# First two groups of a layer multiplied by x in one VectorE instruction, and two whole chunks in place of four

## The chip, the cores and the metric

The kernel runs on one core of a Trainium2 chip. The metric is the device time of one execution in microseconds, the median of several runs. All five engines of the core share its SBUF; the matrix results lie in PSUM.

## The reference

The input x has 512 samples of 39 fields with 32 components each. Three layers follow one another; each forms all products of the fields with the hidden rows of the layer before, component by component, multiplies them by a weight matrix, adds a bias and takes the positive part. Half of the 200 outputs of layers 0 and 1 is hidden input of the next layer, the other half goes to the result; layer 2 gives all 200. The result is summed over the 32 components.

```
hidden = x
for i in range(3):
    z = einsum('bmd,bnd->bmnd', x, hidden).reshape(B, -1, D)
    cur = relu(einsum('bcd,co->bod', z, Ws[i]) + bs[i][None, :, None])
    hidden, direct = (cur[:, :100], cur[:, 100:]) if i < 2 else (cur, cur)
    finals.append(direct)
y = concatenate(finals, axis=1).sum(-1)
```

All inputs and outputs are 32-bit floats.

## The kernel before

A **unit** is one of the 4 tiles of 128 samples at one of the 32 components: 128 units. For each unit the products of a layer are laid out in **chunks** of 128 rows by 128 samples: 7 chunks in layer 0, 31 chunks in each of layers 1 and 2 (39 fields by 100 hidden rows). The 31 chunks are worked on in four **groups** of 8, 8, 8 and 7 (`GROUP`, `GROUPS`, `group_chunks`).

Each group, and layer 0 as one, is a numbered batch that passes through four steps:

- VectorE multiplies hidden rows by x into one slot of `z` (three slots, `RING`) (`product12`, for layer 0 `product0`), and counts the semaphore `product`.
- ScalarE copies the slot, rounded, into `z_high` (`highs`; four buffers), after `product` has reached the batch.
- VectorE subtracts `z_high` from `z` into `z_low` (`lows`; three buffers). It waits for `high` of this batch, then for `freed`: the multiplication three batches before must have ended.
- TensorE multiplies each chunk twice (`multiply`): `z_high` by the high and low halves of the weights (400 columns, L812), and `z_low` by the high half (200 columns, L813). This makes a nearly full-precision product out of a faster number format.

`WHOLE` chunks at the front of layer 2 don't take this way. They are multiplied in full 32-bit form, once, from `z_whole` and `w_whole` (L805); so group 0 of layer 2 has 4 whole and 4 split chunks, and its `highs` and `lows` run over 4 chunks. `z_whole` lies in front of the three slots of `z`, so that one instruction writes the whole and the split part when the batch has slot 0.

The order on each engine is written out by hand in `period`. A period takes layer 1 of unit n, layer 0 of unit n+2 and layer 2 of unit n-1, nine batches in all. On VectorE, P is a product, L a `lows`, the number is the batch within the period:

```
P0 L(-1) P1 L0 P2 L1 P3 L2 sums2 P4 directs L3 P5 L4 P6 L5 P7 L6 P8 L7 sums
```

Batches 0 to 3 are layer 1, 4 is layer 0, 5 to 8 are layer 2. TensorE takes the batches in their order, two transposes at the period's end. ScalarE takes `highs` 0 to 8 in order; before `highs` 3 it makes the hidden rows of layer 2 (`second_half2`, `hidden(1, ...)`), before `highs` 5 those of layer 1 (`hidden(0, ...)`). `slot_read` makes a product wait until the `lows` three batches before has ended. SyncE loads x, repeated over the partitions, for the next unit: after P5 has ended the chunks of group 0 (`load_xb`: L284 for partitions 0 to 95, L291 for the rest), after P6 those of group 1, and so on; layer 1's product of the next unit waits for them on `xb_in[g]`. There are two buffers of x.

In the last two units layer 0 is absent, so that slots fall otherwise; there, and in the closing part after the loop, group 0 of layer 2 is multiplied in two instructions (L464 and L468).

Of the kernel before, what the change touches and what calls it, by code (L numbers as in the profile page):

```python
# [10 lines left out]
P = 128  # L11
# [41 lines left out]
TAIL_AT = GROUP * (GROUPS - 1)  # L53


WHOLE = 4


RING, HIGH_RING = 3, 4
# [9 lines left out]
def group_chunks(g):  # L69
    return min(GROUP, CHUNKS - GROUP * g)  # L70


def split_from(layer, g):
    return WHOLE if (layer, g) == (2, 0) else 0


def split_chunks(layer, g):
    return group_chunks(g) - split_from(layer, g)


# [21 lines left out]
def cin_kernel(nc, r_x, W0, W1, W2, b0, b1, b2, out):  # L102
# [6 lines left out]
    with ExitStack() as ctx:  # L109
# [81 lines left out]


        def stage(l, g):
            at, n = g % 2 * STAGED, split_chunks(l, g)
            return mixed[:, at:at + n * O].rearrange("p (c o) -> p c o", o=O)

        z_all = z_both
# [27 lines left out]

        def piece(l, g):
            at = GROUP * g + split_from(l, g) - (WHOLE if l == 2 else 0)
            return w_split[l][:, at:at + split_chunks(l, g), :]

        def load_w(queue, l, g, w, bias):  # L230
            k = GROUPS * (l - 1) + g
            skip, n = split_from(l, g), split_chunks(l, g)
            a = GROUP * g + skip
            wt, row = w.tensor, HID * O
            st = stage(l, g)
            if skip:
                queue.dma_start(w_whole[0:MAIN, :, :], bass.AP(wt, 0, [[O, MAIN], [row, skip], [1, O]])).then_inc(w_whole_in, 16)
                queue.dma_start(w_whole[MAIN:P, :, :], bass.AP(wt, CHUNKS * row, [[O, P - MAIN], [row, skip], [1, O]])).then_inc(w_whole_in, 16)
            queue.dma_start(st[0:MAIN, :, :], bass.AP(wt, a * row, [[O, MAIN], [row, n], [1, O]])).then_inc(w_in[k], 16)
            if g < GROUPS - 1:  # L240
                queue.dma_start(st[MAIN:P, :, :],
                                bass.AP(wt, (CHUNKS + skip) * row + 32 * g * O, [[O, P - MAIN], [row, n], [1, O]])).then_inc(w_in[k], 16)
            else:
                queue.wait_ge(stage_ready, l)
                full = F // TAIL_CHUNKS
                at = MAIN + TAIL * full
                for t in range(TAIL):
                    queue.dma_start(st[MAIN + t:at:TAIL, 0:TAIL_CHUNKS, :],
                                    bass.AP(wt, (MAIN + t) * O, [[TAIL_CHUNKS * row, full], [row, TAIL_CHUNKS], [1, O]])).then_inc(w_in[k], 16)
                queue.dma_start(st[at:at + TAIL, 0:F - TAIL_CHUNKS * full, :],  # L250
                                bass.AP(wt, TAIL_CHUNKS * full * row + MAIN * O, [[O, TAIL], [row, F - TAIL_CHUNKS * full], [1, O]]))\
                     .then_inc(w_in[k], 16)
                queue.dma_start(st[ONES_ROW:ONES_ROW + 1, 0, :], bass.AP(bias.tensor, 0, [[O, 1], [1, O]])).then_inc(w_in[k], 16)
# [160 lines left out]
        def _(dve):  # L414
# [25 lines left out]
            def product0(u, number, slot):  # L440
# [3 lines left out]
                dst = z[0:L0_ROWS, slot % RING, 0:L0_CHUNKS * T].rearrange("p (c t) -> p c t", t=T)  # L444
                nc.vector.tensor_tensor(dst, left, x_right[0:L0_ROWS, :, :], ALU.mult).then_inc(product, 1)  # L445

            def product12(layer, u, par, g, number, slot):
                slot_read(number)
                if g == 0:
                    dve.wait_ge(hid_in[layer], u + 1)  # L450
                if layer == 1:
                    dve.wait_ge(xb_in[g], xb_count(u))
                    if isinstance(u, int) and u < 2:
                        dve.wait_ge(repeats_in[u], HALVES * Q)
                n, c0 = group_chunks(g), GROUP * g
                dst = z[:, slot % RING, 0:n * T].rearrange("p (c t) -> p c t", t=T)
                left = hid[layer][:, par, g, :].unsqueeze(1).to_broadcast([P, n, T])
                if split_from(layer, g):

                    if not (isinstance(u, int) and u == 0):  # L460
                        dve.wait_ge(whole_used, u)
                    dst = z_both[:, 0:n * T].rearrange("p (c t) -> p c t", t=T)
                    if slot % RING:
                        nc.vector.tensor_tensor(dst[:, 0:WHOLE, :], left[:, 0:WHOLE, :], xb[par][:, 0:WHOLE, :], ALU.mult)  # L464
                        n, c0 = n - WHOLE, WHOLE
                        dst = z[:, slot % RING, 0:n * T].rearrange("p (c t) -> p c t", t=T)
                        left = left[:, WHOLE:, :]
                nc.vector.tensor_tensor(dst, left, xb[par][:, c0:c0 + n, :], ALU.mult).then_inc(product, 1)  # L468

            def lows(number, slot, rows, n):  # L470
                dve.wait_ge(high, number + 1)
# [96 lines left out]
            def period(r, d, n, base, sl):  # L568

                par = d % 2  # L570
                second, final = (r, d) == (0, 1), (r, d) == (TILES - 1, D - 1)
                a, b = layers_ended(r, d)

                def slot(p):
                    return sl + p

                product12(1, n, par, 0, base, slot(0))
                if not second:
                    lows(base - 1, slot(-1), P, group_chunks(3))
                product12(1, n, par, 1, base + 1, slot(1))  # L580
                lows(base, slot(0), P, group_chunks(0))
                if second:
                    sums(0, 2, ended(0), 2)
                    low_piece(5, 2, 0)
                product12(1, n, par, 2, base + 2, slot(2))
                lows(base + 1, slot(1), P, group_chunks(1))
                product12(1, n, par, 3, base + 3, slot(3))
                if second:
                    low_piece(6, 2, 1)
                    dve.wait_ge(w_low_done, 7)  # L590
                    stage_zeros(2)
                lows(base + 2, slot(2), P, group_chunks(2))
                if not second:
                    sums2(n - 2)
                q = 4
                if a == 0:
                    product0(n + 2, base + 4, slot(4))
                directs(r, d, n)
                if a == 0:
                    lows(base + 3, slot(3), P, group_chunks(3))  # L600
                    q = 5
                if second:
                    low_piece(7, 2, 2)
                product12(2, n - 1, 1 - par, 0, base + q, slot(q))
                if a == 0:
                    lows(base + 4, slot(4), L0_ROWS, L0_CHUNKS)
                else:
                    lows(base + 3, slot(3), P, group_chunks(3))
                product12(2, n - 1, 1 - par, 1, base + q + 1, slot(q + 1))
                lows(base + q, slot(q), P, split_chunks(2, 0))  # L610
                product12(2, n - 1, 1 - par, 2, base + q + 2, slot(q + 2))
                lows(base + q + 1, slot(q + 1), P, group_chunks(1))
                if second:
                    low_piece(8, 2, 3)
                if final:
                    sums(a, b, ended(n), n + 2)
                product12(2, n - 1, 1 - par, 3, base + q + 3, slot(q + 3))
                lows(base + q + 2, slot(q + 2), P, group_chunks(2))
                if not final:
                    sums(a, b, ended(n), n + 2)  # L620
# [11 lines left out]

            at = first(UNITS)
            lows(at - 1, at - 1, P, group_chunks(3))
            product12(2, UNITS - 1, 1, 0, at, at)
            sums2(UNITS - 2)
            for g in range(1, GROUPS):
                product12(2, UNITS - 1, 1, g, at + g, at + g)
                lows(at + g - 1, at + g - 1, P, split_chunks(2, g - 1))
            lows(at + 3, at + 3, P, group_chunks(3))  # L640
            dve.wait_ge(s_in, ended(UNITS - 1))
# [10 lines left out]
        def _(act):  # L652
# [73 lines left out]
            def period(r, d, n, base, sl):  # L726
# [33 lines left out]
                if turn:  # L760
                    for bank in range(X_BANKS):
                        turned_x(r + 1, bank)
                highs(base + q + 1, slot(q + 1), P, group_chunks(1))
                if second:
                    high_piece(2, 3)
                if final:
# [29 lines left out]
        @block.tensor  # L796
        def _(pe):
            def multiply(layer, number, slot, g=0):
                c0, n = (0, L0_CHUNKS) if layer == 0 else (GROUP * g + split_from(layer, g), split_chunks(layer, g))
                rows, chunks = (L0_ROWS, L0_CHUNKS) if layer == 0 else (P, CHUNKS)  # L800
                a = acc[:, layer, :]
                if split_from(layer, g):
# [60 lines left out]
            def period(r, d, n, base, sl):  # L863
# [21 lines left out]
                    pe.wait_ge(s2_in, n - 1)  # L885
                for g in range(GROUPS):
                    if second:
                        pe.wait_ge(w_low_done, 2 + GROUPS + g)
                        if g == 0:
                            pe.wait_ge(w_whole_in, 32)  # L890
                    if final and g == GROUPS - 1:
                        transpose(a, b, ended(n))
                    multiply(2, base + q + g, slot(q + g), g)
# [43 lines left out]
```

## Time and profile before

| | |
|---|---|
| median of 3 runs | 2717.37 us (2715.43 to 2718.66) |
| profiled execution | 2715.79 us, of which the span is 2714.0 us |
| TensorE (PE) busy | 2674.4 us, 99% of the span |
| VectorE (DVE) busy | 2646.5 us, 98% |
| ScalarE (ACT) busy | 1673.1 us, 62% |
| DMA | 123 GB/s mean |
| granted TensorE clock | 0.994 of full speed |

Busy time is the time in which at least one instruction of the engine runs. The profile gives a start and a duration for each instruction; on VectorE the next instruction can start a little before the one in front of it has ended, so the distance from start to start (called the step below) is shorter than the duration. A releaser in brackets behind an instruction names what ended the idle time in front of it.

### The profile page before, as it was taken

To read this page: it belongs to the slowest core of one execution; us is meant where nothing else is said; L and a number is where in the kernel's file an instruction comes from. 1 tells how busy PE (TensorE), PEld (TensorE's weight loads), DVE (VectorE), ACT (ScalarE), POOL (GpSimd) and SP (SyncE) were. 2 spreads that over 40 slices of the span, in tenths; PEclk is the share of its full clock that TensorE was granted. 3 is DMA by queue.
4 is the path that set the end of the run, shared out by engine and by line. 5 is a ranking of instruction groups with operands and counts; after the bars stand their busy time and mean duration, and the time that the engine had idled before them with its cause. 6 is when DMAs were issued, how large, how long until landed. Compare 5 with 4: busy or idle time off the path is not lost.

```text
span 2714.0 us, 52144 instructions
## 1 busy us (share of the span) xinstructions
PE 2674.4 (99%) x17992; PEld 2660.7 (98%) x17992; DVE 2646.5 (98%) x2736; ACT 1673.1 (62%) x2850; POOL 0.7 (0%) x7
## 2 busy tenths in 40 slices
PE   6899999999999999999999999999999999999999
PEld 4899999999999999999999999999999999999999
DVE  6999999999999999999999999999999999999998
ACT  4566666666666666666666666666666666666664
POOL 0000000000000000000000000000000000000000
PEclk8999999999999999999999999999999999999999
DMA  7544544444455444444445544444454444444442
GB/s 184 137 130 115 131 121 110 126 130 111 117 143 136 110 123 131 112 114 131 122 123 136 133 114 112 130 123 110 122 131 118 114 131 123 110 123 132 111 110 63
DMA packets 230130, 332.65 MB, mean 123 GB/s; under 512 B 27976, under 2 KB 165172, under 8 KB 229940
## 3 DMA queue, kind: packets, MB, share of 16 engines
q1 hardware_dynamic: 230038, 331.46, 46.6%
q8 instruction: 54, 0.88, 0.1%
q14 instruction: 38, 0.31, 0.0%
HBM read 326.67 MB, written 6.60 MB: 123 GB/s over the span
## 4 chain that ended last, share of the span: by engine, by line
PE 98%; DVE 1%; ACT 1%; issue 0%; DMA 0%; SPq 0%; DVEq 0%; ACTq 0%
PE acc L812 61%; PE acc L813 28%; PE acc L805 6%; PE turned L825 1%; PE x_turned L848 1%; DVE z_low L473 0%; DVE w_split L418 0%; ACT w_split L691 0%; ACT z_high L656 0%; PE x_turned L834 0%; DMA mixed<-in_r_x_dram 0%; DVE z L468 0%; ACT mixed L681 0%; DVE z L445 0%; ACT mixed L678 0%
## 5 line engine op out<-in xcount | busy, mean ns | idle before, releaser
L812 PE MATMUL acc<-w_split,z_high 128*128 128x400 f32 (+1 forms) x8320 | 2493.5, 367 | 27.2 <-DVE z_low L473 25.9
L813 PE MATMUL acc<-w_split,z_low 128*128 128x200 f32 (+1 forms) x8320 | 2120.5, 255 | 0.0
L812 PEld LDWEIGHTS acc<-w_split,z_high 128*128 128x128 f32 (+1 forms) x8320 | 1565.5, 188 | 30.1 <-issue 17.7
L813 PEld LDWEIGHTS acc<-w_split,z_low 128*128 128x128 f32 (+1 forms) x8320 | 1593.0, 191 | 0.0
L656 ACT ACTIVATE z_high<-z 128x1024 fp32r<-128x1024 f32 (+3 forms) x1152 | 1112.4, 975 | 705.4 <-DVE z L468 584.6
L473 DVE TENSOR_TENSOR z_low<-z,z_high 128x1024 fp32r<-128x1024 f32 (+3 forms) x1152 | 1284.8, 1115 | 27.3 <-PE acc L813 25.6
L468 DVE TENSOR_TENSOR z<-mixed,xb 128x1024 f32<-128x1024 f32 (+2 forms) x1024 | 1211.7, 1183 | 1.8 <-ACT mixed L681 1.8
L681 ACT ACTIVATE mixed<-turned 32x128 f32<-32x128 f32 x768 | 204.5, 266 | 8.9
L805 PE MATMUL acc<-w_whole,z 128*128 128x200 f32 x1024 | 196.6, 335 | 1.4 <-DVE s L487 1.4
L805 PEld LDWEIGHTS acc<-w_whole,z 128*128 128x128 f32 x1024 | 168.1, 190 | 1.7 <-DVE s L487 1.7
L678 ACT ACTIVATE mixed<-turned 96x512 f32<-96x512 f32 x256 | 150.9, 590 | 9.5 <-PE turned L825 4.6
L661 ACT ACTIVATE half<-acc 128x400 f32<-128x400 f32 (+1 forms) x130 | 64.8, 498 | 122.9 <-PE acc L813 122.9
L445 DVE TENSOR_TENSOR z<-x_left,x_right 118x896 f32<-118x896 f32 x128 | 138.5, 1082 | 0.1
L666 ACT ACTIVATE half<-acc 128x200 f32<-128x200 f32 x128 | 43.2, 338 | 99.0 <-PE acc L813 99.0
L481 DVE TENSOR_TENSOR s<-acc,half 128x400 f32<-128x400 f32 (+1 forms) x130 | 73.0, 561 | 3.1 <-ACT half L661 3.1
L671 ACT ACTIVATE s<-s 128x48 f32<-128x48 f32 (+1 forms) x130 | 31.4, 242 | 71.2 <-DVE s L481 71.2
L494 DVE SCALAR_TENSOR_TENSOR direct<-s,direct 128x400 f32<-128x400 f32 (+2 forms) x133 | 72.0, 541 | 0.3
L679 ACT ACTIVATE mixed<-turned 32x128 f32<-32x128 f32 x256 | 69.2, 270 | 3.0
L825 PE MATMUL turned<-s 128*128 128x128 f32 x256 | 49.4, 273 | 1.1 <-ACT s L671 1.1
L487 DVE TENSOR_TENSOR s<-acc,half 128x200 f32<-128x200 f32 x128 | 45.9, 359 | 3.9 <-ACT half L666 3.9
L825 PEld LDWEIGHTS turned<-s 128*128 128x128 f32 x256 | 29.9, 141 | 1.5 <-ACT s L671 1.5
L418 DVE TENSOR_TENSOR w_split<-mixed,w_split 128x1600 fp32r<-128x1600 f32 (+2 forms) x8 | 13.3, 1666 | 6.5 <-ACT w_split L691 6.5
(27 smaller groups left out, 79.1 us busy)
## 6 DMA issues: line engine op xcount, KB each, us to landing
xb<-x_by_unit SPq DMA_DIRECT2D x378, 384.0 KB, 4.2
x_right<-x_by_unit SPq DMA_DIRECT2D x384, 136.5 KB
xb<-x_by_unit SPq DMA_DIRECT2D x384, 128.0 KB, 4.9
xb<-x_by_unit SPq DMA_DIRECT2D x126, 336.0 KB
xb<-x_by_unit SPq DMA_DIRECT2D x128, 84.0 KB
x_left<-x_by_unit SPq DMA_DIRECT2D x384, 19.5 KB
mixed<-in_L_rec_W_dram SPq DMA_DIRECT2D x5, 600.0 KB, 5.5
x_by_unit<-mixed SPq DMA_DIRECT2D x16, 160.0 KB, 2.8
```

The source lines that it names most:

```text
L445: nc.vector.tensor_tensor(dst, left, x_right[0:L0_ROWS, :, :], ALU.mult).then_inc(product, 1)
L468: nc.vector.tensor_tensor(dst, left, xb[par][:, c0:c0 + n, :], ALU.mult).then_inc(product, 1)
L473: nc.vector.tensor_tensor(z_low[slot % RING][0:rows, 0:n * T], z[0:rows, slot % RING, 0:n * T], z_high[slot % HIGH_RING][0:rows, 0:n * T]. ...
L481: nc.vector.tensor_tensor(s[:, a:b, :, 0:HID], acc[:, a:b, 0:O].rearrange("p l (h o) -> p l h o", o=HID), half[:, a:b, :, :], ALU.add).the ...
L494: return nc.vector.scalar_tensor_tensor(direct[:, a:b, :], s[:, a:b, 1, 0:HID], 0.0, direct[:, a:b, :], ALU.max, ALU.add)
L656: nc.scalar.activation(z_high[slot % HIGH_RING][0:rows, 0:n * T], z[0:rows, slot % RING, 0:n * T], ACT.Copy).then_inc(high, 1)
L678: nc.scalar.activation(h[0:MAIN, :, :], t[0:MAIN, :].unsqueeze(1).to_broadcast([MAIN, GROUPS, T]), ACT.Relu)
L681: last = nc.scalar.activation(h[MAIN:P, g, :], t[32 * g:32 * (g + 1), :], ACT.Relu)
L805: used = nc.tensor.matmul(a[:, 0:O], z_whole[:, c * T:(c + 1) * T], w_whole[:, c, :], start=(c == 0), stop=False, skip_group_check=True)
L812: nc.tensor.matmul(a[:, 0:2 * O], z_high[slot % HIGH_RING][0:rows, tok], w, start=(c == 0), stop=False, skip_group_check=True)
L813: last = nc.tensor.matmul(a[:, 0:O], z_low[slot % RING][0:rows, tok], w[:, 0:O], start=False, stop=(c == chunks - 1), skip_group_check=True)
L825: last = nc.tensor.transpose(turned[:, 0, l * P:(l + 1) * P], s[:, l, 0, :], ident)
```

## The change

`WHOLE` goes from 4 to 2. The batches of layer 2 are cut anew: batch 5 is chunks 2 to 9, batch 6 chunks 10 to 15, the others as before; 8, 6, 8 and 7 split chunks in place of 4, 8, 8 and 7. In each full period P0 and P1 become one instruction over 16 chunks (`product_two`), and so do P5 and P6; both raise `product` by two when they end. It waits for the slots of both batches, for x of both groups in layer 1, and it stands where P0 and P5 stood. The order becomes

```
P01 L(-1) L0 P2 L1 P3 L2 sums2 P4 directs L3 P56 L4 L5 P7 L6 P8 L7 sums
```

Where the slot of batch 5 isn't slot 0 (the last two units and the closing part) four instructions take the place of P5 and P6. The first unit's layer 1 keeps its own code. The loading of the weights follows the new cut, with 2 whole and 6 split chunks in the first piece of layer 2.

```diff
-WHOLE = 4
+WHOLE = 2
...
+def batch_chunks(layer, g):
+    at = GROUP * g + (WHOLE if layer == 2 and g < 2 else 0)
+    end = GROUP * (g + 1) + (WHOLE if layer == 2 and g == 0 else 0)
+    return at, min(end, CHUNKS) - at
+
+def split_chunks(layer, g):
+    return batch_chunks(layer, g)[1]
...
-def split_chunks(layer, g):
+def piece_chunks(layer, g):
     return group_chunks(g) - split_from(layer, g)
...
+            def product_two(layer, u, par, number, slot):
+                slot_read(number + 1)
+                dve.wait_ge(hid_in[layer], u + 1)
+                x_ready(layer, u, 0)
+                x_ready(layer, u, 1)
+                at = slot % RING
+                left = hid[layer][:, par, 0:2, :].unsqueeze(2).to_broadcast([P, 2, GROUP, T])
+                x = xb[par][:, 0:2 * GROUP, :].rearrange("p (g c) t -> p g c t", g=2)
+                if layer == 2 and not (isinstance(u, int) and u == 0):
+                    dve.wait_ge(whole_used, u)
+                if layer == 1 or at == 0:
+                    assert at + 2 <= RING
+                    c = 0 if layer == 2 else WHOLE + GROUP * at
+                    dst = z_both[:, c * T:(c + 2 * GROUP) * T].rearrange("p (g c t) -> p g c t", g=2, t=T)
+                    nc.vector.tensor_tensor(dst, left, x, ALU.mult).then_inc(product, 2)
+                    return
+                def part(to, g, a, b):
+                    return nc.vector.tensor_tensor(to.rearrange("p (c t) -> p c t", t=T), left[:, g, a:b, :], x[:, g, a:b, :], ALU.mult)
+                one, two = z[:, at, :], z[:, (at + 1) % RING, :]
+                rest = GROUP - WHOLE
+                part(z_whole, 0, 0, WHOLE)
+                part(one[:, 0:rest * T], 0, WHOLE, GROUP)
+                part(one[:, rest * T:], 1, 0, WHOLE).then_inc(product, 1)
+                part(two[:, 0:rest * T], 1, WHOLE, GROUP).then_inc(product, 1)
...
-                product12(1, n, par, 0, base, slot(0))
+                product_two(1, n, par, base, slot(0))
                 if not second:
                     lows(base - 1, slot(-1), P, group_chunks(3))
-                product12(1, n, par, 1, base + 1, slot(1))
                 lows(base, slot(0), P, group_chunks(0))
...
-                product12(2, n - 1, 1 - par, 0, base + q, slot(q))
+                product_two(2, n - 1, 1 - par, base + q, slot(q))
                 if a == 0:
                     lows(base + 4, slot(4), L0_ROWS, L0_CHUNKS)
...
-                product12(2, n - 1, 1 - par, 1, base + q + 1, slot(q + 1))
                 lows(base + q, slot(q), P, split_chunks(2, 0))
...
-                        pe.wait_ge(w_low_done, 2 + GROUPS + g)
+                        pe.wait_ge(w_low_done, 2 + GROUPS + max(g, 1))
```

## Rows read from the trace of the kernel before

**Rows 1.** The page: busy time of the engines, and the last chain by engine.

```profile
PE 2674.4 (99%) x17992; PEld 2660.7 (98%) x17992; DVE 2646.5 (98%) x2736; ACT 1673.1 (62%) x2850; POOL 0.7 (0%) x7
...
PE 98%; DVE 1%; ACT 1%; issue 0%; DMA 0%; SPq 0%; DVEq 0%; ACTq 0%
```

**Rows 2.** Timeline of VectorE, early periods: start us, duration us, instruction, [idle before <-releaser].

```profile
163.91 1.08 DVE L445 TENSOR_TENSOR z<-x_left,x_right 118x896 f32<-118x896 f32 x1
184.26 1.08 DVE L445 TENSOR_TENSOR z<-x_left,x_right 118x896 f32<-118x896 f32 x1
...
192.00 1.23 DVE L473 TENSOR_TENSOR z_low<-z,z_high 128x1024 fp32r<-128x1024 f32 x1 [0.17 <-PE acc L813]
...
212.64 1.22 DVE L473 TENSOR_TENSOR z_low<-z,z_high 128x1024 fp32r<-128x1024 f32 x1 [0.20 <-PE acc L813]
```

**Rows 3.** Timeline of VectorE, one late period, from sums2 to L6.

```profile
1506.61 0.36 DVE L487 TENSOR_TENSOR s<-acc,half 128x200 f32<-128x200 f32 x1
1506.89 1.08 DVE L445 TENSOR_TENSOR z<-x_left,x_right 118x896 f32<-118x896 f32 x1
...
1509.38 1.22 DVE L468 TENSOR_TENSOR z<-mixed,xb 128x1024 f32<-128x1024 f32 x1
1510.51 1.09 DVE L473 TENSOR_TENSOR z_low<-z,z_high 118x896 fp32r<-118x896 f32 x1
1511.51 1.22 DVE L468 TENSOR_TENSOR z<-mixed,xb 128x1024 f32<-128x1024 f32 x1
1512.65 0.68 DVE L473 TENSOR_TENSOR z_low<-z,z_high 128x512 fp32r<-128x512 f32 x1
...
1514.67 1.22 DVE L473 TENSOR_TENSOR z_low<-z,z_high 128x1024 fp32r<-128x1024 f32 x1 [0.20 <-PE acc L813]
```

**Rows 4.** Groups by line and shape: count | busy us, mean ns | idle before.

```profile
L468 DVE TENSOR_TENSOR z<-mixed,xb 128x1024 f32<-128x1024 f32 x765 | 932.0, 1218 | 1.8 <-ACT mixed L681 1.8
...
L468 DVE TENSOR_TENSOR z<-mixed,xb 128x896 f32<-128x896 f32 x256 | 277.7, 1085 | 0.0
```

**Rows 5.** Timeline of TensorE, from layer 0's last chunk into batch 5.

```profile
1516.17 0.36 PE L812 MATMUL acc<-w_split,z_high 118*128 118x400 f32 x1
...
1516.46 1.53 PE L805 MATMUL acc<-w_whole,z 128*128 128x200 f32 x8
1517.69 0.49 PE L812 MATMUL acc<-w_split,z_high 128*128 128x400 f32 x1
...
1518.11 0.36 PE L812 MATMUL acc<-w_split,z_high 128*128 128x400 f32 x1
```

**Rows 6.** Timelines of VectorE and of ScalarE: P2 and its copy; end of `hidden(0, ...)`.

```profile
1502.20 1.22 DVE L468 TENSOR_TENSOR z<-mixed,xb 128x1024 f32<-128x1024 f32 x1
```

```profile
1503.46 1.06 ACT L656 ACTIVATE z_high<-z 128x1024 fp32r<-128x1024 f32 x1 [1.15 <-DVE z L468]
...
1509.97 0.82 ACT L681 ACTIVATE mixed<-turned 32x128 f32<-32x128 f32 x3
```

**Rows 7.** Timelines of ScalarE and of VectorE at the start: a subtraction waits for its copy.

```profile
29.22 0.95 ACT L656 ACTIVATE z_high<-z 118x896 fp32r<-118x896 f32 x1 [2.88 <-DVE z L445]
```

```profile
30.21 1.09 DVE L473 TENSOR_TENSOR z_low<-z,z_high 118x896 fp32r<-118x896 f32 x1 [1.08 <-ACT z_high L656]
```

**Rows 8.** Timeline of VectorE: instructions that wait for the one right in front.

```profile
40.29 1.23 DVE L430 MEMSET mixed<- 32x1400 f32 x1 [0.35 <-DVE w_split L418]
...
2662.45 0.36 DVE L487 TENSOR_TENSOR s<-acc,half 128x200 f32<-128x200 f32 x1
2662.94 0.57 DVE L494 SCALAR_TENSOR_TENSOR direct<-s,direct 128x400 f32<-128x400 f32 x1
```

**Rows 9.** SyncE's issue for group 1 of x, its landing (source view), the next P0.

```profile
1513.30 0.38 SPq L291 DMA_DIRECT2D xb<-x_by_unit  x1
```

```profile
DMA to landing us min/median/max: 4.5/4.5/4.5
```

```profile
1518.44 1.22 DVE L468 TENSOR_TENSOR z<-mixed,xb 128x1024 f32<-128x1024 f32 x1
```

More of the change, by code:

```diff
@@ L193, in stage @@
         def stage(l, g):
-            at, n = g % 2 * STAGED, split_chunks(l, g)
+            at, n = g % 2 * STAGED, piece_chunks(l, g)
             return mixed[:, at:at + n * O].rearrange("p (c o) -> p c o", o=O)
@@ L227, in piece @@
             at = GROUP * g + split_from(l, g) - (WHOLE if l == 2 else 0)
-            return w_split[l][:, at:at + split_chunks(l, g), :]
+            return w_split[l][:, at:at + piece_chunks(l, g), :]
         def load_w(queue, l, g, w, bias):
             k = GROUPS * (l - 1) + g
-            skip, n = split_from(l, g), split_chunks(l, g)
+            skip, n = split_from(l, g), piece_chunks(l, g)
             a = GROUP * g + skip
@@ L445, in product0, with x_ready @@
                 nc.vector.tensor_tensor(dst, left, x_right[0:L0_ROWS, :, :], ALU.mult).then_inc(product, 1)
+            def x_ready(layer, u, g):
+                if layer == 1:
+                    dve.wait_ge(xb_in[g], xb_count(u))
+                    if isinstance(u, int) and u < 2:
+                        dve.wait_ge(repeats_in[u], HALVES * Q)
             def product12(layer, u, par, g, number, slot):
@@ L450, in product12 @@
                     dve.wait_ge(hid_in[layer], u + 1)
[L451 to L454, printed above, removed]
+                x_ready(layer, u, g)
                 n, c0 = group_chunks(g), GROUP * g
@@ L457, in product12 @@
                 left = hid[layer][:, par, g, :].unsqueeze(1).to_broadcast([P, n, T])
[L458 to L467, printed above, removed]
@@ L608, in period @@
                     lows(base + 3, slot(3), P, group_chunks(3))
-                product12(2, n - 1, 1 - par, 1, base + q + 1, slot(q + 1))
                 lows(base + q, slot(q), P, split_chunks(2, 0))
                 product12(2, n - 1, 1 - par, 2, base + q + 2, slot(q + 2))
-                lows(base + q + 1, slot(q + 1), P, group_chunks(1))
+                lows(base + q + 1, slot(q + 1), P, split_chunks(2, 1))
                 if second:
@@ L634, in _ @@
             lows(at - 1, at - 1, P, group_chunks(3))
-            product12(2, UNITS - 1, 1, 0, at, at)
+            product_two(2, UNITS - 1, 1, at, at)
             sums2(UNITS - 2)
             for g in range(1, GROUPS):
-                product12(2, UNITS - 1, 1, g, at + g, at + g)
+                if g > 1:
+                    product12(2, UNITS - 1, 1, g, at + g, at + g)
                 lows(at + g - 1, at + g - 1, P, split_chunks(2, g - 1))
@@ L762, in period @@
                         turned_x(r + 1, bank)
-                highs(base + q + 1, slot(q + 1), P, group_chunks(1))
+                highs(base + q + 1, slot(q + 1), P, split_chunks(2, 1))
                 if second:
@@ L798, in multiply @@
             def multiply(layer, number, slot, g=0):
-                c0, n = (0, L0_CHUNKS) if layer == 0 else (GROUP * g + split_from(layer, g), split_chunks(layer, g))
+                c0, n = (0, L0_CHUNKS) if layer == 0 else batch_chunks(layer, g)
                 rows, chunks = (L0_ROWS, L0_CHUNKS) if layer == 0 else (P, CHUNKS)
```

## The prediction

> **What bounds the kernel now.** I read the page first: TensorE and VectorE are both busy for all but 1 to 2% of the span, and the last chain lies on TensorE for 98% of it [rows 1]. Shares so close don't say which engine has room, so I went to VectorE's timeline. In the early periods VectorE waits for nobody, and layer 0's product comes every 184.26 - 163.91 = 20.35 us; that is VectorE's own period. From 192 us on it meets a wait for TensorE (`freed`) once a period, at L6, and the distance becomes 212.64 - 192.00 = 20.64 us [rows 2]. That is TensorE's period, and it holds to the end: the same wait stands in a late period [rows 3]. So TensorE sets the pace, VectorE runs as far ahead as three `z_low` buffers allow, and its room is 20.64 - 20.35 = 0.29 us per period. Whatever adds more than 0.29 us to VectorE's period makes VectorE the bound, and each 0.01 us beyond that costs 1.24 us over the 124 full periods from unit 2 to unit 125. The reader is to see that this number is small against one wait.
>
> **TensorE's side.** A split chunk takes 1516.46 - 1516.17 = 0.29 us. The four whole chunks take from 1516.46 to 1517.69, and the chunk behind them starts its successor 0.42 us later in place of 0.29, so 1.23 + 0.13 = 1.36 us, 0.34 each [rows 5]. Two whole chunks turned into two split ones save about 2 x 0.05 = 0.10 us: TensorE's period becomes about 20.54 us. If TensorE stays the bound, this is the whole effect.
>
> **VectorE's instructions.** Between 896 and 1024 elements the mean goes from 1085 to 1218 ns [rows 4]: 1.04 ns per element. A product of 1024 elements has a step of 1.14 us (1511.51 to 1512.65 [rows 3]), of which 1.07 is elements and 0.07 is fixed. A product over 2048 elements isn't in the trace; from these it has a step of 1.14 + 1.07 = 2.20 us (unrounded) and a duration of 1.218 + 1.066 = 2.28 us. Two merges save 2 x 0.07 = 0.14 us per period. It could save nothing, if the added dimension costs as much as a start; that would be 0.14 more, and is inside the range. The subtractions of batches 5 and 6 go from 4 + 8 to 8 + 6 chunks: 256 elements more, 256 x 1.04 = 0.27 us. Instructions alone: 20.35 - 0.14 + 0.27 = 20.48 us. That would still fit under TensorE.
>
> **The new wait on ScalarE, twice a period.** Before, a product and another subtraction stood between a product and its own subtraction. Now only L(-1), or L4, does. Let P01 start at 0. It ends at 2.28. ScalarE starts the copy 0.04 later (P2 ends at 1502.20 + 1.22 = 1503.42, the copy starts at 1503.46) and takes 1.06 us [rows 6]: 3.38. A subtraction that waits for its copy starts 0.04 after it (29.22 + 0.95 = 30.17 against 30.21 [rows 7]): 3.42. VectorE would have come there at 2.20 + 1.00 = 3.20 (1.00 is the step of an 896-element subtraction, 1510.51 to 1511.51 [rows 3]). So it stands 0.21 us (unrounded) before L0, and the same before L5, since L4 has 896 elements too: 0.42 us. ScalarE has nothing else to do at either place: the dup of the last sums is over before P01 ends, and `hidden(0, ...)`, the work in front of copy 5, was over at 1509.97 + 0.82 = 1510.79 [rows 6], while P56 would end at 1509.38 + 0.21 + 2.28 = 1511.87. Behind L0 wait P2 and all else of the in-order queue.
>
> **The new wait on VectorE itself, once a period.** `product_two` in layer 2 needs both slots, so it waits for L3 to end, and L3 is the instruction right in front of it (before, only L2 had to be over). In layer 1 L(-2) has the sums behind it, and the wait is free. The trace has such waits outside the steady part: L494 waits for L487 and starts 0.49 us after it, where L487's step without a wait is 0.28 [rows 8, 3]: 0.21 us. L430 behind L418 stands 0.35 us, plus the 0.08 by which steps are shorter than durations: 0.43 us [rows 8]. Nothing is the bound from below, if the engine empties anyway. I take 0.21, the row nearest in kind: three waits in a row and an ordinary tensor instruction, as here. A rule speaks for less: the Trainium skill (VectorE: DVE Perf Modes, "The DRAIN you can't avoid") says that the next operation can't start until the pipe is empty and that a semaphore after each operation "costs nothing extra here". This trace disagrees, with 0.49 us against 0.28 for the same instruction. By the rule this term would be 0, and the result is the first rival.
>
> **Sum.** 20.48 + 0.42 + 0.21 = 21.11 us: 0.47 over 20.64, with VectorE the bound. TensorE needs 20.54 and waits about 0.57 us in each period. Following the batches through such a period, the tightest place is batch 4, whose subtraction ends latest against TensorE; nowhere is `freed` late, as TensorE is then never three batches behind. 124 x 0.47 = 58.3 us. At the ends: the second unit's first weight piece has 6 chunks in place of 4 (0.4 us on VectorE) and P56 of that period is behind the same chain, together 0.7 us. The last two units and the closing part have four product instructions for three, the two extra chunks and one new wait each, about 1 us in all. Against that, TensorE ends closer behind VectorE: its backlog at batch 4 was 2.8 us (L4 ended at 1510.51 + 1.09 = 1511.60; the seven chunks ended at 1516.46, so they began 7 x 0.29 before, at 1514.4) [rows 3, 5]; it is used up once, which gives back about 1.9 us at the end. Net -0.2: 58 us. The profiled execution took 2715.8 us, the median of the runs is 1.6 above it: 2715.8 + 58 + 1.6 = 2775 us, 2.1% slower.
>
> **x arrives later.** The loads of groups 0 and 1 now both start after P56. The last of group 1 was issued 0.57 us after P6's end (1511.51 + 1.22 = 1512.73 to 1513.30) and landed 4.5 us on, at 1517.80, for a use at 1518.44 + 1.14 + 1.00 = 1520.58 [rows 9, 3]: 2.8 us of room. Now four issues stand behind one product, so this one comes some 1.6 us after P56's end and lands 6.1 after it. The next P01 comes L4's remainder, L5 with its wait, P7, L6, P8, L7 and sums later, 6.9 us after P56's end. Room: 0.8 us. I cost it at nothing; the cover is thin.
>
> **The rivals.**
> - *The wait on itself is free.* Period 20.90, 124 x 0.26 = 32 us: 2749. For it: the rule above; against it: rows 8.
> - *x is late.* If group 1 lands over 0.8 us later than worked out, P01 of the next unit waits. Each 0.1 us too late costs 12 us: with 0.2 us, 2800. For it: the transfers of both groups, 1 MB, queue together; against it: the period is longer and other loads keep their place.
> - *TensorE stays the bound* (the other side). If VectorE's additions stay under 0.19 us in sum (20.54 - 20.35), the period falls to 20.54 and 124 x 0.10 = 12 us are gained: 2705. This needs both waits on ScalarE and the one on itself to vanish: the copy would have to be done 0.21 us sooner than its own duration allows. What could be thought to carry them, the backlog of 2.8 us in the three buffers, is spent in 2.8 / 0.47 = 6 periods.
> - *Between*: additions of 0.19 to 0.31 us leave the time within 0.2%.
>
> **How the numbers follow.** Forecast 2775: 0.67. Wait on itself free: 0.10. x late: 0.16. TensorE stays the bound: 0.04. Between: 0.03. The range goes from the first rival's 2748 to 2804, which is the forecast with 0.43 for the wait on itself (124 x 0.22 = 27 more), and holds most of the second rival. A measurement tells about 0.2% (5 us) from no change; faster 0.04, same 0.03, slower 0.93.
>
> **What would show it.** Step to step of L445: 21.1 us. Idle before L473 with ScalarE's copy as releaser, 0.1 to 0.2 us, about 250 times; the waits of L473 for TensorE all but gone; TensorE waiting for `z_low` once a period, about 0.57 us, some 70 us in all. The product over 2048 elements at 2.28 us. An idle of 0.13 us or so before P56. A wait of P01 for x would show the second rival. The prediction is wrong if the period stays at 20.5 to 20.6, or if the copies turn out to end before VectorE asks for them.

## The result and the profile after

The changed kernel takes 2792.01 us in the median (2789.47 to 2793.99, 5 runs) against 2717.29 us: the ratio is 1.0276, with a 95% interval of 1.0262 to 1.029. It is slower by 75 us where 58 were forecast, and inside the range. The profiled execution took 2792.01 us with a span of 2790.2, 76.2 more than before.

Line numbers have moved: L813 is L846, L812 is L845, L805 is L838 for TensorE; L473 is now L507 (`lows`), L468 is L473 (single products), L491 is the merged product, L445 is L457 (layer 0's), L487 is L521, L494 is L528, L481 is L515 (sums), L656 is L689 (the copies), L291 is L303.

The page of the changed kernel, to be held against [rows 1]:

```profile
PE 2705.8 (97%) x17992; PEld 2653.7 (95%) x17992; DVE 2690.6 (96%) x2487; ACT 1684.6 (60%) x2850; POOL 0.7 (0%) x7
...
PE 85%; DVE 7%; issue 7%; ACT 1%; DMA 0%; DVEq 0%; SPq 0%; ACTq 0%
```

No engine is busier in share than before, though the kernel is slower. In time VectorE is busy for 44.1 us more (the added subtractions, and gaps too short for the view to show) and idle for 32.1 us more. The chain still names TensorE for 85%. It only leaves TensorE where that waited, so it doesn't tell who sets the pace. The waits do (us in total, times, longest), and so do the groups by shape (count | busy us, mean ns | idle before):

```profile
PE acc L845 <- DVE z_low L507: 68.7, 141, 7.9
...
DVE z_low L507 <- ACT z_high L689: 13.2, 61, 1.2
...
DVE z L491 <- DMA xb<-x_by_unit: 9.7, 18, 1.2
```

```profile
L491 DVE TENSOR_TENSOR z<-mixed,xb 128x2048 f32<-128x2048 f32 x252 | 577.0, 2290 | 24.2 <-DMA xb<-x_by_unit 9.7 <-ACT mixed L714 1.9
...
L845 PE MATMUL acc<-w_split,z_high 118*128 118x400 f32 x896 | 287.9, 381 | 56.8 <-DVE z_low L507 56.8
```

TensorE waits for `z_low` 68.7 us, 56.8 of them at layer 0's batch, and VectorE's waits for TensorE are gone. Of the 68.7, some 25 us are waits at the start that the kernel before had too (25.9 us in all); from 140 us on the view shows 43.6 us. It shows a wait only in part, as TensorE's timeline at layer 0's first chunks has it:

```profile
1727.55 0.37 PE L845 MATMUL acc<-w_split,z_high 128*128 128x400 f32 x1
...
1728.32 0.45 PE L845 MATMUL acc<-w_split,z_high 118*128 118x400 f32 x1 [0.31 <-DVE z_low L507]
...
1728.71 0.36 PE L845 MATMUL acc<-w_split,z_high 118*128 118x400 f32 x1
```

The steps are 0.77 and 0.39 us in place of 0.29 each: 0.58 us lost, of which 0.31 stands as idle.

The merged product takes 2.29 us, 2.28 worked out. One period of VectorE inside a loop, the timeline from L3 to P7, is to be held against [rows 3] (L4 and L5 share one line, `x2`):

```profile
1532.08 1.09 DVE L507 TENSOR_TENSOR z_low<-z,z_high 128x896 fp32r<-128x896 f32 x1
1533.26 2.29 DVE L491 TENSOR_TENSOR z<-mixed,xb 128x2048 f32<-128x2048 f32 x1
1535.46 2.44 DVE L507 TENSOR_TENSOR z_low<-z,z_high 118x896 fp32r<-118x896 f32 x2
1537.82 1.22 DVE L473 TENSOR_TENSOR z<-mixed,xb 128x1024 f32<-128x1024 f32 x1
```

From L3 to P56 it is 1533.26 - 1532.08 = 1.18 us where the step is 1.00: the wait on itself costs 0.18. From L4 to P7, 1537.82 - 1535.46 = 2.36 us hold two subtractions, L4 and L5, whose steps are 1.00 and 1.14: the wait for the copy costs 0.22. It doesn't show as idle time, as the view joins gaps this short. Outside the loops the same place is longer, and there the view shows it:

```profile
1500.14 2.29 DVE L491 TENSOR_TENSOR z<-mixed,xb 128x2048 f32<-128x2048 f32 x1
1502.35 1.08 DVE L507 TENSOR_TENSOR z_low<-z,z_high 128x896 fp32r<-128x896 f32 x1
1503.62 1.23 DVE L507 TENSOR_TENSOR z_low<-z,z_high 128x1024 fp32r<-128x1024 f32 x1 [0.19 <-ACT z_high L689]
```

```profile
1502.53 2.01 ACT L689 ACTIVATE z_high<-z 128x1024 fp32r<-128x1024 f32 x2 [2.14 <-DVE z L491]
```

The product ends at 1500.14 + 2.29 = 1502.43, the copy starts at 1502.53, and L0 starts 1.27 us after L(-1) in place of 1.00.

The third thing is late x. A late period: VectorE's timeline at the sums and P01, then SyncE's issue of the last load of group 1 and its landing.

```profile
1563.05 0.57 DVE L515 TENSOR_TENSOR s<-acc,half 128x400 f32<-128x400 f32 x1
1563.95 2.29 DVE L491 TENSOR_TENSOR z<-mixed,xb 128x2048 f32<-128x2048 f32 x1 [0.33 <-DMA xb<-x_by_unit]
```

```profile
1558.30 0.38 SPq L303 DMA_DIRECT2D xb<-x_by_unit  x1
```

```profile
DMA to landing us min/median/max: 5.5/5.5/5.5
```

1558.30 + 5.5 = 1563.8, and P01 starts 0.15 us behind that, 0.90 us after the sums' start in place of 0.48.

The distance between layer 0's products, over the 123 periods from 105.01 to 2717.04 us, is 21.236 us in the mean, against 20.644 before: 72.9 us. The most frequent, and the shortest that comes again, is 21.08 in the loops of the program (96 periods); outside, where the periods are written out one by one, about 21.20. The rest of the 76.2 lies at the ends: 2.1 us before the first of these products, 1.3 after the last.

### The profile page after: what moved, and what is told of

It reads as the page before. It is cut to its first block, busy times and chain, and to the rows that moved or that the text cites. A ratio compares the mean times of both kernels' runs of the same rounds, so it can differ in the third digit from the quotient of the medians.

```text
span 2790.2 us, 51923 instructions
## 1 busy us (share of the span) xinstructions
PE 2705.8 (97%) x17992; PEld 2653.7 (95%) x17992; DVE 2690.6 (96%) x2487; ACT 1684.6 (60%) x2850; POOL 0.7 (0%) x7
## 3 DMA queue, kind: packets, MB, share of 16 engines
q1 hardware_dynamic: 230038, 331.46, 44.1%
## 4 chain that ended last, share of the span: by engine, by line
PE 85%; DVE 7%; issue 7%; ACT 1%; DMA 0%; DVEq 0%; SPq 0%; ACTq 0%
PE acc L845 55%; PE acc L846 25%; DVE z_low L507 6%; PE acc L838 3%; PE turned L858 1%; PE x_turned L881 1%; ACT w_split L724 0%; ACT z_high L689 0%; DVE w_split L430 0%; PE x_turned L867 0%; DVE z L495 0%; DVE z L473 0%; DMA mixed<-in_r_x_dram 0%; ACT mixed L714 0%; DVE z L457 0%
## 5 line engine op out<-in xcount | busy, mean ns | idle before, releaser
L845 PE MATMUL acc<-w_split,z_high 128*128 128x400 f32 (+1 forms) x8576 | 2597.6, 369 | 70.8 <-DVE z_low L507 68.7
L846 PE MATMUL acc<-w_split,z_low 128*128 128x200 f32 (+1 forms) x8576 | 2186.4, 255 | 0.0
L845 PEld LDWEIGHTS acc<-w_split,z_high 128*128 128x128 f32 (+1 forms) x8576 | 1615.0, 188 | 111.9 <-DVE z_low L507 89.5
L689 ACT ACTIVATE z_high<-z 128x1024 fp32r<-128x1024 f32 (+3 forms) x1152 | 1125.8, 998 | 961.7 <-DVE z L473 437.3
L846 PEld LDWEIGHTS acc<-w_split,z_low 128*128 128x128 f32 (+1 forms) x8576 | 1643.3, 192 | 0.0
L507 DVE TENSOR_TENSOR z_low<-z,z_high 128x1024 fp32r<-128x1024 f32 (+3 forms) x1152 | 1319.7, 1146 | 37.4 <-ACT z_high L689 13.2
L491 DVE TENSOR_TENSOR z<-mixed,xb 128x2048 f32<-128x2048 f32 x252 | 577.0, 2290 | 24.2 <-DMA xb<-x_by_unit 9.7
L473 DVE TENSOR_TENSOR z<-mixed,xb 128x1024 f32<-128x1024 f32 (+1 forms) x514 | 592.2, 1152 | 0.0
L457 DVE TENSOR_TENSOR z<-x_left,x_right 118x896 f32<-118x896 f32 x128 | 138.4, 1082 | 0.1
L838 PE MATMUL acc<-w_whole,z 128*128 128x200 f32 x512 | 110.5, 339 | 2.6 <-DVE s L521 2.6
L838 PEld LDWEIGHTS acc<-w_whole,z 128*128 128x128 f32 x512 | 82.2, 191 | 2.9 <-DVE s L521 2.9
L515 DVE TENSOR_TENSOR s<-acc,half 128x400 f32<-128x400 f32 (+1 forms) x130 | 73.0, 562 | 1.6 <-ACT half L694 1.6
L528 DVE SCALAR_TENSOR_TENSOR direct<-s,direct 128x400 f32<-128x400 f32 (+2 forms) x133 | 71.9, 541 | 0.3
L521 DVE TENSOR_TENSOR s<-acc,half 128x200 f32<-128x200 f32 x128 | 45.9, 359 | 4.9 <-ACT half L699 4.9
```

Source lines behind the costliest of these rows:

```text
L491: nc.vector.tensor_tensor(dst, left, x, ALU.mult).then_inc(product, 2)
L507: nc.vector.tensor_tensor(z_low[slot % RING][0:rows, 0:n * T], z[0:rows, slot % RING, 0:n * T], z_high[slot % HIGH_RING][0:rows, 0:n * T]. ...
L515: nc.vector.tensor_tensor(s[:, a:b, :, 0:HID], acc[:, a:b, 0:O].rearrange("p l (h o) -> p l h o", o=HID), half[:, a:b, :, :], ALU.add).the ...
L689: nc.scalar.activation(z_high[slot % HIGH_RING][0:rows, 0:n * T], z[0:rows, slot % RING, 0:n * T], ACT.Copy).then_inc(high, 1)
L838: used = nc.tensor.matmul(a[:, 0:O], z_whole[:, c * T:(c + 1) * T], w_whole[:, c, :], start=(c == 0), stop=False, skip_group_check=True)
L845: nc.tensor.matmul(a[:, 0:2 * O], z_high[slot % HIGH_RING][0:rows, tok], w, start=(c == 0), stop=False, skip_group_check=True)
```

## Experiments

Late x is measured in each run by one thing: the distance from the start of sums to the start of the product behind it, less 0.485 us, added up over the profiled execution. It is 0 in the kernel before and 14.7 us in the changed kernel. It is read from one execution per kernel, while the medians are of several, and executions of these kernels differ by 2 to 13 us (`directs_after_l4`: 2770.5 to 2783.2), so differences of a few us in late x are not clear of that. Undisturbed means the shortest period that comes again and again, in the loops. All ratios are to the kernel before, run beside each, with 95% intervals.

| run | median us | ratio | undisturbed period | late x, us |
|---|---|---|---|---|
| before | 2716.2 to 2717.3 | 1 | 20.64 | 0 |
| changed | 2792.0 | 1.0276 | 21.08 | 14.7 |
| pairs_later | 2790.0 | 1.0271 (1.0254 to 1.0288) | 21.08 | 11.0 |
| directs_before_two | 2785.0 | 1.026 (1.0243 to 1.0277) | 20.90 | 26.2 |
| directs_after_l4 | 2778.7 | 1.0231 (1.0207 to 1.0255) | 20.87 | 24.4 |
| x_not_reloaded | 2777.1 | 1.0223 (1.0207 to 1.0239) | 21.08 | 0 |
| whole_only | 2712.3 | 0.9984 (0.9975 to 0.9994) | 20.61 | 0 |
| whole_three | 2711.5 | 0.9979 (0.997 to 0.9989) | 20.59 | 0 |
| merge_layer1 | 2745.5 | 1.01 (1.0084 to 1.0116) | 20.76 | 10.2 |
| merge_layer2 | 2757.0 | 1.0145 (1.0129 to 1.0161) | 20.94 | 0 |
| merge_four_whole | 2776.9 | 1.0224 (1.0207 to 1.0241) | 20.81 | 29.7 |
| merge_layer2_filled | 2709.2 | 0.9969 (0.9959 to 0.998) | 20.54 | 0 |

### Is x late because of the loads in front of it?

```diff
-                if not (r == TILES - 1 and d >= D - 3):
-                    sp.wait_ge(product, at + GROUPS + 1)
-                    load_pairs(n + 3)
                 for g in range(GROUPS):
                     ...
                         load_xb(n + 1, 1 - d % 2, g)
+                if not (r == TILES - 1 and d >= D - 3):
+                    sp.wait_ge(product, at + GROUPS + 1)
+                    load_pairs(n + 3)
```

> The changed kernel with layer 0's loads (load_pairs) issued after the four loads of x in place of before them. Theory that late x made the rest (the undisturbed period is 21.08 us in the loops and 21.2 outside, the mean is 21.24, and 18 waits for x stand in the trace): without the pair loads in front, x of groups 0 and 1 lands in time, the mean period falls to about 21.11, 123 x 0.13 = 16 us less, 2776 us, and no wait for x is left. Rival, that the longer periods come from something else and the waits for x are only where it shows: 2792 us, the same spread of periods.

Missed, for the most part. Late x went from 14.7 to 11.0 us only, and the medians are 2 us apart. The waits that remain:

```profile
DVE z L491 <- DMA xb<-x_by_unit: 5.6, 9, 1.8
```

The loads of layer 0 in front account for a quarter of it at most; with one execution each, even this 3.7 us isn't clear of the spread.

### Is x late at all the reason?

```diff
-                    if not (r == TILES - 1 and d == D - 1):
+                    if g > 1 and not (r == TILES - 1 and d == D - 1):
                         sp.wait_ge(product, at2 + g + 1)
...
-                if layer == 1:
+                if layer == 1 and (g > 1 or isinstance(u, int) and u < 2):
                     dve.wait_ge(xb_in[g], xb_count(u))
```

> The changed kernel without the loads of groups 0 and 1 of x from unit 2 on, and without the waits for them; both buffers keep the chunks of units 0 and 1 there, so this part of the product is of other x, all else is the same. Theory that late x made all of the spread: the distance from sums to P01 is 0.48 us in each period, periods are 21.08 in the loops and 21.20 outside, mean 21.11, so 123 x 0.13 = 16 us less, 2776 us. Rival, that the spread comes from ScalarE or from semaphores: 2792 us.

This kernel leaves out the loads, so that what it computes is wrong. As expected: 2777.1 us, mean period 21.111 us, late x 0, each period in the loops 21.07 to 21.14. So 15 us of the changed kernel's 75 are late x, and what remains is the forecast's period of 21.11 us to the hundredth.

### The wait of the product for the instruction in front

```diff
-                directs(r, d, n)
-                if a == 0:
                     lows(base + 3, slot(3), P, group_chunks(3))
                     q = 5
+                directs(r, d, n)
```

> The changed kernel with directs moved from in front of L3 to between L3 and P56, so that L3 isn't right in front of the product that waits for it. Theory that the wait on itself costs 0.18 us (L3 to P56 is 1.18 us in the trace against a step of 1.00): 123 x 0.18 = 22 us less, 2770 us, step of L528 before P56 at 0.49. Rival, that the engine empties between any two instructions and the wait costs nothing: 2792 us.

VectorE's timeline from L3 on:

```profile
1715.66 1.09 DVE L507 TENSOR_TENSOR z_low<-z,z_high 128x896 fp32r<-128x896 f32 x1
1716.66 0.57 DVE L528 SCALAR_TENSOR_TENSOR direct<-s,direct 128x400 f32<-128x400 f32 x1
1717.14 2.29 DVE L491 TENSOR_TENSOR z<-mixed,xb 128x2048 f32<-128x2048 f32 x1
```

L3's step is 1.00 and directs' 0.48, so the wait is gone, and the undisturbed period fell from 21.08 to 20.90, by the 0.18 us of the theory. The time didn't follow: 7 us in the median (9 between the two profiled executions) in place of 22. Late x took 11.5 of the rest, 26.2 us where it was 14.7. The expectation had left that out.

### What L5 waits for

```diff
-                directs(r, d, n)
-                if a == 0:
                     lows(base + 3, slot(3), P, group_chunks(3))
                     q = 5
+                else:
+                    directs(r, d, n)
...
                 if a == 0:
                     lows(base + 4, slot(4), L0_ROWS, L0_CHUNKS)
+                    directs(r, d, n)
```

> The changed kernel with directs moved to between L4 and L5, where VectorE waits for ScalarE's copy. Theory that the copy is what L5 waits for: directs (0.485 us) fills the wait of 0.21 to 0.27 us, and as the next P01 comes 0.27 us later after P56, x is late less often: 26 us less from the wait and up to 8 from x, 2758 to 2766 us. Rival, that L5 waits for something else that moves along with it: 2792 us.

```profile
1711.27 1.08 DVE L507 TENSOR_TENSOR z_low<-z,z_high 118x896 fp32r<-118x896 f32 x1
1712.27 0.57 DVE L528 SCALAR_TENSOR_TENSOR direct<-s,direct 128x400 f32<-128x400 f32 x1
1712.76 1.22 DVE L507 TENSOR_TENSOR z_low<-z,z_high 128x1024 fp32r<-128x1024 f32 x1
```

Directs runs with its bare step of 0.49, and L5 follows without a wait. The undisturbed period fell by 0.21 us, the wait for one copy; 123 x 0.21 = 26 us. 13 came back in the median, 17 between the profiled executions; late x took most of the rest, some 10. 2778.7 us is outside the expected 2758 to 2766, as the part on x is wrong: late x grew to 24.4 us, though P01 is due 7.17 us after P56's end where it was 6.90. P56 had moved closer behind P4 and the pair loads by 0.48 us, which could explain it; that is argued and not shown.

### Each part of the change by itself

Two whole chunks alone, in the kernel before:

```diff
-WHOLE = 4
+WHOLE = 2
```

> The kernel before with WHOLE = 2 and nothing else: 6, 8, 8 and 7 split chunks in layer 2, no merged product. Theory: VectorE's own period is 20.35 + 0.27 = 20.62 us and TensorE's falls by 0.10 to 20.54, so VectorE just about takes over as the bound and the time stays within 4 us of 2717. Rival, that the two more chunks in subtractions are what made the changed kernel slow: well above 2730 us.

Period 20.61 us with 20.62 expected, and 2712.3 us, 3.9 below the kernel before that ran beside it. The two added chunks don't make the change slow. Three whole chunks (`WHOLE = 3`):

> The kernel before with WHOLE = 3 alone. Theory: VectorE's own period is 20.35 + 0.13 = 20.48 and TensorE's 20.64 - 0.05 = 20.59 us, so TensorE stays the bound: 123 x 0.05 = 6 us under before, 2711 us. Rival: VectorE is the bound at all values of WHOLE, then 20.48 and 2697 us.

Period 20.59 us, 2711.5, as expected. TensorE is the bound here, at the 0.05 us per chunk read from [rows 5], and VectorE with two whole chunks. ScalarE's waits for TensorE tell them apart, first with three, then with two:

```profile
ACT half L661 <- PE acc L813: 118.5, 127, 3.7
```

```profile
ACT half L661 <- PE acc L813: 7.2, 3, 3.2
```

In the kernel before this wait was 122.9 us.

Layer 1's merge on `WHOLE = 2`, layer 2's products as in `whole_only` (`product_two` itself is left out here):

```diff
-                product12(1, n, par, 0, base, slot(0))
+                product_two(1, n, par, base, slot(0))
                 if not second:
                     lows(base - 1, slot(-1), P, group_chunks(3))
-                product12(1, n, par, 1, base + 1, slot(1))
```

> WHOLE = 2, layer 1's two groups merged, layer 2's not (batches of 6, 8, 8, 7). Theory: one saved start and one wait for the copy: 20.61 - 0.07 + 0.21 = 20.75 us in the loops, 0.11 over before, 123 x 0.11 = 14 us: 2730; and since P01 needs group 1 of x a product and a subtraction sooner than before, with some 0.9 us of room as in the changed kernel, late x adds up to 15 us: 2730 to 2745. Rival, that x is late because both groups are loaded at once after P56: then no wait for x here, 2730.

And layer 2's merge, which is the changed kernel with P0 and P1 of layer 1 as two products again, L(-1) between them:

> WHOLE = 2, layer 2's two groups merged, layer 1's not. Theory: one saved start, one wait for the copy, one wait of the product for L3: 20.61 - 0.07 + 0.21 + 0.18 = 20.93 us, 0.29 over before, 123 x 0.29 = 36 us: 2752 to 2756; no wait for x, since P0 needs group 0 alone. Rival, that the loads of both groups at once are late by themselves: waits for x, and 2765 or more.

The first: period 20.76 with 20.75 expected, 2745.5 us at the upper end of the 2730 to 2745, late x 10.2 us, with waits in the trace (the merged product is L488 there) although groups 0 and 1 are loaded one after the other, as in the kernel before:

```profile
DVE z L488 <- DMA xb<-x_by_unit: 7.2, 13, 1.5
```

The second: period 20.94 with 20.93 expected, no late x, 2757.0 us (2752 to 2756 expected). So the wait for x comes with layer 1's merge, which asks for group 1 a product and a subtraction sooner; both loads being issued at once, as in the second, doesn't bring it by itself. Against `whole_only`, the two merges cost 33 and 45 us; together 78, and the changed kernel is 80 over it.

Both merges with four whole chunks, the changed kernel with `WHOLE = 4`:

> The changed kernel with WHOLE = 4: both merges, 8, 4, 8 and 7 split chunks in layer 2. Theory: 256 elements fewer in the subtractions take 0.27 us off the undisturbed period, 21.08 to 20.81 us in the loops; but the same 0.27 us lie between P56 and the next P01, the room that x has, so late x grows from 15 us to 35 or more: 123 x 0.27 = 33 less and some 25 more, 2775 to 2790 us. Rival, that late x doesn't depend on that room: 2759 us.

```profile
DVE z L491 <- DMA xb<-x_by_unit: 22.5, 60, 1.4
```

The period is 20.81 us as expected, 33 us less in sum, but the time fell by 15, inside the expected 2775 to 2790. Late x doubled to 29.7 us (35 or more expected), with 60 waits in place of 18: shortening VectorE's work between the load and its use eats half of its own gain.

### A version that keeps the saved start

Layer 2's merge only, as above, with `sums2` taken from behind L2 to between L3 and P56, and `directs` from in front of L3 to between L4 and L5:

```diff
-                if not second:
+                if not second and a != 0:
                     sums2(n - 2)
...
-                directs(r, d, n)
-                if a == 0:
                     lows(base + 3, slot(3), P, group_chunks(3))
+                    if not second:
+                        sums2(n - 2)
                     q = 5
+                else:
+                    directs(r, d, n)
...
                 if a == 0:
                     lows(base + 4, slot(4), L0_ROWS, L0_CHUNKS)
+                    directs(r, d, n)
```

> merge_layer2 with other work in both holes: sums2 between L3 and P56, directs between L4 and L5. Theory: both waits are covered and only the saved start is left: VectorE's own period 20.61 - 0.07 = 20.54 us, about TensorE's 20.54: 123 x 0.10 = 12 us under before, 2703 to 2707 us, and faster than WHOLE = 2 alone (2712). Rival, that TensorE's period with two whole chunks is really 20.61: 2712 us, as WHOLE = 2 alone.

VectorE's timeline, L3 to L5:

```profile
1505.47 1.08 DVE L507 TENSOR_TENSOR z_low<-z,z_high 128x896 fp32r<-128x896 f32 x1
1506.47 0.36 DVE L521 TENSOR_TENSOR s<-acc,half 128x200 f32<-128x200 f32 x1
1506.75 2.28 DVE L491 TENSOR_TENSOR z<-mixed,xb 128x2048 f32<-128x2048 f32 x1
1508.95 1.08 DVE L507 TENSOR_TENSOR z_low<-z,z_high 118x896 fp32r<-118x896 f32 x1
1509.95 0.57 DVE L528 SCALAR_TENSOR_TENSOR direct<-s,direct 128x400 f32<-128x400 f32 x1
1510.44 1.22 DVE L507 TENSOR_TENSOR z_low<-z,z_high 128x1024 fp32r<-128x1024 f32 x1
```

Every step is bare: 1.00, 0.28, 2.20, 1.00, 0.49. The period is 20.54 us, and the median 2709.2 us is below both kernels and some 3 us below `whole_only`, the same kernel without the merge. It is 2 to 6 us over what was expected; about 3 of these lie in eight periods of 20.6 to 21.1 us outside the loops or at their edges. In three of them VectorE waited 0.26 to 0.41 us for a copy of ScalarE; the rest is open.

## Why the prediction was right, and where it was off

- **What bounds.** Right: 0.29 us of room, passed at once, and TensorE waits once a period at layer 0's batch. The size is right where it is read from steps: 0.58 us in the period above, 0.57 forecast. That the waits view sums to 68.7 us where 70 were forecast is luck: some 25 of them lie at the start and were there before, and it shows only about half of each wait in the loops.
- **Period.** 21.11 us forecast, 21.111 measured once x is taken out. Its terms: the merged product 2.28 us against 2.29; the wait for the copy 0.21 against 0.21 in the loops (by `directs_after_l4`) and 0.27 outside; the wait on itself 0.21 against 0.18 (by `directs_before_two`). The two small misses cancel (21.08 in the loops, 21.20 outside), so the agreement to the hundredth is partly luck. The idle in front of the subtractions was to show about 250 times and shows 61 times, as the view joins the shorter gaps in the loops.
- **The rule on the pipe.** The Trainium skill (VectorE: DVE Perf Modes, "The DRAIN you can't avoid") has a semaphore behind an operation cost nothing extra. The first rival rested on that, and it fell, as this case's traces disagree: an instruction that waits for the one right in front starts 0.18 us later than one that doesn't, 1.18 us after L3's start against 1.00.
- **x arrives later.** This is the step that failed: "I cost it at nothing; the cover is thin". It measured 15 us, the greater part of the 17 missing. The place and the sign were right, and the second rival had the wait; it came on top of the forecast. Of the terms behind the room of 0.8 us two hold: in 22 periods in a row (1537 to 1982 us) the last load of group 1 was issued 1.5 to 1.9 us after P56's end, 1.6 worked out, and P01 was due 6.9 us after it. The landing doesn't: it was taken from one load at 4.5 us [rows 9], and in these periods it took 4.3 to 6.2 us, 5.0 in the middle. The trace of the kernel before could have told: between 600 and 2600 us its loads of this line took 3.6 to 6.5 us, 4.9 in the middle (3.1, 6.8 and 4.9 in the changed kernel). Another 0.1 to 0.2 us pass between the landing and P01's start. And a wait is one-sided: early landings give nothing back for late ones, so room in the mean still costs when single landings spread over more than that. The rival's reason, that both transfers queue together, isn't borne out as enough by itself (`merge_layer2` has no late x, `merge_layer1` has it without).
- **The ends.** Forecast -0.2 us in sum, measured +3.4: 2.1 at the start (0.7 forecast) and 1.3 at the end (-0.9). What makes them is open.
- **The range.** Its upper end by the stated sum is 2775 + 27 = 2802, not 2804, and the first rival's time is 2749 in one place and 2748 in another; neither changes a reading.
- **TensorE stays the bound**, the rival on the other side, fell as stated: it needed less than 0.19 us of additions, and they came to 0.76. That TensorE's period would be 20.54 us wasn't contradicted: `merge_layer2_filled` has that period, but VectorE's own work is as long there, so this shows only that TensorE needs no more.

## What to carry to other kernels

Merging two steps of an in-order pipeline saves one start, here 0.07 us, and holds back the first result by the length of the second half. Count what still lies between the merged instruction and its first user: here one subtraction of 1.00 us stood in front of a copy of 1.06 us plus its two handovers, and 0.21 us of waiting took the place of 0.07 saved. If work that depends on neither can be moved into the hole, the merge pays, here by some 3 us of 2712; merges that make a load due sooner need the spread of its landings, not their middle.

## What the runs showed of the hardware that wasn't expected

The handover from VectorE to ScalarE differs between code in a loop and code written out. Behind the 252 merged products of the changed kernel the copy starts 0.03 to 0.04 us after the product's end in 192, as many as lie in the loops, and 0.09 to 0.10 us after it in the other 60; a wait is 0.06 us shorter in the loops. The kernel before has it too, where it costs nothing: P0 and its copy outside the loops, in the timelines of VectorE and ScalarE,

```profile
1352.33 1.22 DVE L468 TENSOR_TENSOR z<-mixed,xb 128x1024 f32<-128x1024 f32 x1
```

```profile
1353.64 1.06 ACT L656 ACTIVATE z_high<-z 128x1024 fp32r<-128x1024 f32 x1 [0.95 <-DVE z L468]
```

are 1353.64 - 1353.55 = 0.09 us apart, against 0.04 in [rows 6]. No run tried why.

And shortening the period of the changed kernel raised late x each time (0.18 us off: 15 to 26 us; 0.21 off: to 24; 0.27 off: to 30), even where the time from P56's end to P01 stayed (6.89 us, `directs_before_two`) or grew (7.17, `directs_after_l4`). What in the transfers makes their landings spread is open; the pair loads in front are a quarter of it at most.
